# Rotary self-attention of a two-layer perceiver: units reordered by half of the tokens, output summed over heads in PSUM, scores on 64 keys instead of 128

## The chip, the cores and the metric

One core of a Trainium2 chip runs the whole program: TensorE (PE in the profile; its weight loads are PEld), VectorE (DVE), ScalarE (ACT), GpSimd (POOL) and SyncE (SP, which only issues DMAs here). The metric is the device time of one execution in microseconds, median of several runs.

## The reference, cut to what matters

The program is two layers, each of cross-attention, self-attention and a feed-forward net, on 16 batches of 64 tokens with 256 features. The change touches one block only, the self-attention of layer 1:

```python
N_HEADS, D_MODEL, D_HEAD = (16, 256, 128)
# x: (16, 64, 256), normalised; per head h:
q, k, v = xn @ W_Q[h] + b_Q[h], xn @ W_K[h] + b_K[h], xn @ W_V[h] + b_V[h]
q, k = apply_rope(q, cos, sin), apply_rope(k, cos, sin)
p = softmax(causal(q @ k.T / sqrt(128)))       # within one batch: 64 x 64
x += sum over h of (p @ v) @ W_O[h]  + b_O
```

## The kernel before

The 1024 tokens are 8 tiles of 128 rows; a tile holds two batches of 64. `self_attention_rotary` works in **units**: one head for one half of the tokens (`TH` = 4 tiles, 512 tokens), 32 units in all. Before, unit n is head n // 2 and half n % 2, so two units in a row share the weights of a head.

Every engine runs the same chain of steps 0 to 34 in a software pipeline (`unit_loop`; the order on each engine is written out by hand in its `step`). In step n there stand: the projections of unit n (Q and K with rotation, V), the scores and softmax of unit n - 1, the mix (probabilities times V) of unit n - 2, and the output projection of unit n - 3. Semaphores count finished steps; a wait blocks all that is behind it on its engine.

- PE, step n: `project_to` for Q (six f16 matmuls of 512 columns, since hi and lo parts of both operands are multiplied in three products), scores (f32, one per tile, over all 128 keys of the tile), `project_to` for K, transposes of the probabilities, output projection (12 matmuls), V (24 matmuls), mix.
- DVE: `rope` for Q, mask and row minimum of the scores, `rope` for K, addition of the output projection to `m.x`, reciprocal, `z_lo` (which signals `mix_kept`).
- ACT: in every second step `split_high` (L1694, f16 high part `w_hi` of the next head's weights), then the copy `probs_t` of the transposed probabilities, the four exponentials, the copy of V, `z_hi`.
- POOL: two additions of the rotation, the multiplication of the probabilities by the inverse sum, `split_low` (L1587, `w_lo`).
- SP: `load` fetches the raw weights of a head into one of two buffers `ra_raw` (384 KB), the biases of Q and K, and the bias of V (`ra_v_bias`). The three stand in one queue in this order, each behind its own wait: the raw weights wait for `split_low` two heads back (`w_split`), the Q/K bias for `rope` (`crossing`), the V bias for `z_lo` (`mix_kept`).

The mask is a 128 x 128 table; keys of the other batch of a tile have -1e30 in it. The output projection of each unit goes to its own PSUM group and DVE adds it to `m.x` in every step.

## Time and profile before

| | us |
|---|---|
| median of 3 runs | 900.21 |
| lowest, highest | 896.24, 904.9 |
| span of the profiled execution | 899.1 |
| PE, DVE busy in the span | 758.3, 644.4 |
| ACT, POOL busy in the span | 432.0, 404.5 |
| first weight split of the changed block starts | 597.8 |
| last addition of the block to `m.x` starts | 851.21 |

The profiled execution is one execution. Its own device time is not listed apart; its span, from the first to the last instruction, is 1.1 us under the median of the runs. The changed block takes 254 of the 899 us. Matmuls overlap in PE, so that PE's progress is read from the starts of its rows, not from their durations. In the timeline "x8" merges eight instructions; an f32 matmul appears as two.

### The profile page before, as it was taken

To read this page: it belongs to the slowest core of one execution; us is meant where nothing else is said; L and a number is where in the kernel's file an instruction comes from. 1 tells how busy PE (TensorE), PEld (TensorE's weight loads), DVE (VectorE), ACT (ScalarE), POOL (GpSimd) and SP (SyncE) were. 2 spreads that over 40 slices of the span, in tenths; PEclk is the share of its full clock that TensorE was granted. 3 is DMA by queue.
4 is the path that set the end of the run, shared out by engine and by line. 5 is a ranking of instruction groups with operands and counts; after the bars stand their busy time and mean duration, and the time that the engine had idled before them with its cause. 6 is when DMAs were issued, how large, how long until landed. Compare 5 with 4: busy or idle time off the path is not lost. (4 is left out here: it accounts for less than half of the span.)

```text
span 899.1 us, 17172 instructions
## 1 busy us (share of the span) xinstructions
PE 758.3 (84%) x5344; PEld 518.4 (58%) x5344; DVE 644.4 (72%) x1461; ACT 432.0 (48%) x1269; POOL 404.5 (45%) x318
## 2 busy tenths in 40 slices
PE   5997999677655579999998699868999999999776
PEld 4664666466422345444443467536788888888544
DVE  4356677656378865556556566658999999999767
ACT  2456655142244335454545656315555555555484
POOL 4301444326034227566566444439665656565210
PEclk9998999888868789999999899979999999999979
DMA  9352000000020011111100400001010101001101
GB/s 260 104 173 94 1 0 0 1 1 1 10 82 0 1 55 46 46 47 45 45 1 0 142 1 0 0 18 37 19 35 18 35 18 35 18 18 69 74 0 48
DMA packets 26638, 35.90 MB, mean 40 GB/s; under 512 B 10208, under 2 KB 17888, under 8 KB 25696
## 3 DMA queue, kind: packets, MB, share of 16 engines
q1 hardware_dynamic: 26592, 35.33, 12.6%
q8 instruction: 24, 0.39, 0.2%
q14 instruction: 22, 0.18, 0.1%
HBM read 34.27 MB, written 1.05 MB: 39 GB/s over the span
## 5 line engine op out<-in xcount | busy, mean ns | idle before, releaser
L1260 POOL TENSOR_TENSOR r_turned_lo<-r_turned_q,r_turned_hi 128x1024 f16<-128x1024 f32 x48 | 102.0, 2128 | 67.3 <-ACT r_turned_hi L1387 62.9
L1602 POOL TENSOR_TENSOR ra_direct<-ra_direct,ra_crossed 128x512 f32<-128x512 f32 x64 | 81.5, 1273 | 86.8 <-DVE ra_crossed L1746 86.8
L636 ACT ACTIVATE c_probs<-bank,c_neg_max 128x128 f32<-128x128 f32 x256 | 89.9, 377 | 60.1 <-DVE c_neg_max L688 60.0
L1746 DVE SCALAR_TENSOR_TENSOR ra_crossed<-bank,ra_bias,ra_sin 64x512 f32<-64x512 f32 x128 | 96.0, 750 | 1.9
L655 POOL TENSOR_TENSOR c_probs<-c_probs,c_inverse 128x512 f32<-128x512 f32 x64 | 65.3, 1039 | 70.9 <-DVE c_inverse L670 70.9
L1387 ACT ACTIVATE r_turned_hi<-r_turned_q 128x1024 f16<-128x1024 f32 x48 | 50.7, 1056 | 79.2 <-DVE r_turned_q L1434 79.1
L252 DVE TENSOR_TENSOR l_q_stack<-bank,l_q_stack 64x512 f16<-64x512 f32 (+1 forms) x64 | 44.1, 689 | 53.8 <-ACT l_q_stack L244 52.6
L601 PE MATMUL bank<-l_out_mat,c_ctx_t 128*128 128x256 f32 x256 | 61.8, 385 | 8.5 <-DVE c_ctx_t L699 8.5
L688 DVE TENSOR_REDUCE c_neg_max<-bank 128x4 f32<-128x512 f32 x64 | 41.4, 685 | 27.5 <-PE bank L65 27.5
L1705 ACT ACTIVATE ra_probs_t<-bank 128x512 f32<-128x512 f32 x32 | 19.1, 597 | 85.6 <-PE bank L1651 85.6
L601 PEld LDWEIGHTS bank<-l_out_mat,c_ctx_t 128*128 128x128 f32 x256 | 46.2, 190 | 18.4 <-issue 8.4
L636 ACT ACTIVATION_READ_ACCUMULATOR c_probs<-bank,c_neg_max 128x1 f32 x256 | 55.6, 217 | 0.0
L1710 ACT ACTIVATE ra_probs<-ra_masked,ra_neg_max 128x128 f32<-128x128 f32 x128 | 49.8, 390 | 11.7 <-DVE ra_neg_max L1765 11.3
L65 PE MATMUL bank<-xt_hi,ra_w_hi 128*128 128x512 f16 x128 | 49.3, 385 | 4.3 <-POOL ra_w_lo L1587 4.3
L1746 DVE SCALAR_TENSOR_TENSOR ra_direct<-bank,ra_bias,ra_cos 128x512 f32<-128x512 f32 x64 | 47.8, 746 | 6.7 <-PE bank L65 5.8
L680 DVE COPY c_probs_t<-bank 128x512 f32<-128x512 f32 x64 | 41.5, 685 | 14.7 <-PE bank L592 14.7
L65 PE MATMUL bank<-xt_lo,ra_w_hi 128*128 128x512 f16 x128 | 49.3, 385 | 0.0
L65 PE MATMUL bank<-xt_hi,ra_w_lo 128*128 128x512 f16 x128 | 49.2, 385 | 0.0
L244 ACT ACTIVATE l_q_stack<-bank 64x512 f16<-64x512 f32 (+1 forms) x64 | 37.6, 588 | 22.3 <-PE bank L65 16.8
L1332 PE MATMUL bank<-r_turned_hi,r_fold_hi 128*128 128x512 f16 x96 | 36.6, 382 | 11.2 <-POOL r_turned_lo L1260 11.1
L65 PE MATMUL bank<-kvt_hi,l_q_stack 128*128 (+1 forms) x256 | 35.1, 228 | 11.9 <-ACT c_probs L636 5.6
L100 POOL TENSOR_TENSOR all_rstd<-all_var,minus_half 128x4 f32<-128x4 f32 (+2 forms) x14 | 13.9, 993 | 69.1 <-DVE all_var L94 69.0
(239 smaller groups left out, 2233.7 us busy)
## 6 DMA issues: line engine op xcount, KB each, us to landing
ra_raw<-l_attn_w_dram SPq DMA_DIRECT2D x16, 384.0 KB, 3.0
wq<-l_wq_dram SPq DMA_DIRECT2D x16, 256.0 KB, 2.7
wo<-l_wo_dram SPq DMA_DIRECT2D x16, 256.0 KB, 3.3
wkcq<-l_wkcq_dram SPq DMA_DIRECT2D x16, 192.0 KB, 2.8
ra_wo<-l_attn_wo_dram SPq DMA_DIRECT2D x1, 2048.0 KB, 9.8
wqr<-l_wqr_dram SPq DMA_DIRECT2D x8, 192.0 KB, 3.5
x_res<-x_dram SPq DMA_DIRECT2D x2, 512.0 KB, 4.1
wkv<-l_wkv_dram SPq DMA_DIRECT2D x16, 64.0 KB, 3.0
```

What stands on the lines that cost most here:

```text
L65: mm = nc.tensor.matmul(out, lhs, rhs, start=(n == 0), stop=(n == last))
L252: nc.vector.tensor_tensor(m.q_stack[HD:P, at[0], at[1], :], src[e * HD:(e + 1) * HD], m.q_stack[0:HD, at[0], at[1], :], ALU.subtract).then ...
L601: mm = nc.tensor.matmul(out_bank, ctx_t[:, n, :, :].rearrange("p b s -> p (b s)"), m.out_mat[:, n, :], start=(n == 0), stop=(n == PAIRS - 1))
L636: e = nc.scalar.activation(probs[u][:, n, :], score_bank[q][:, n - q * HP, :], ACT.Exp, bias=neg_max[u][:, n:n + 1], accum_out=total[u][:, ...
L655: nc.gpsimd.tensor_tensor(out=probs[u][:, at, :], in0=probs[u][:, at, :], in1=inverse[u][:, at].unsqueeze(2).broadcast_to([P, HP, L]), op= ...
L680: nc.vector.tensor_copy(probs_t[u][:, at, :], turn_bank[q]).then_inc(turn_kept, 1)
L688: nc.vector.tensor_reduce(neg_max[u][:, at], score_bank[q], AX.X, ALU.max, negate=True).then_inc(maxed, 1)
L1260: nc.gpsimd.tensor_tensor(out=turned_lo[k % NCH][:], in0=turned_q[k % NCH][:], in1=turned_hi[k % NCH][:], op=ALU.subtract).then_inc(turned ...
L1387: nc.scalar.activation(turned_hi[k % NCH][:], turned_q[k % NCH][:], ACT.Copy).then_inc(turned_high, 1)
L1602: nc.gpsimd.tensor_tensor(out=direct[e][k][:], in0=direct[e][k][:], in1=crossed[k][:], op=ALU.add).then_inc(roped, 1)
L1710: ins = nc.scalar.activation(probs[1 - e][:, t, :], masked[1 - e][:, t, :], ACT.Exp, bias=neg_max[1 - e][:, t:t + 1], scale=-1.0, accum_ou ...
L1746: ins = nc.vector.scalar_tensor_tensor(dst[out_lo:out_lo + rows].rearrange("p t (b s) -> p (t b) s", b=2), src[lo:lo + rows], bias[v][lo:l ...
```

## The change

Units are ordered by halves: unit n is head n % 16 of half n // 16. So every unit needs the weights of another head, and each head's weights are loaded and split twice (32 loads of 384 KB, 32 splits on ACT and on POOL; there are now four buffers each for `w_hi` and `w_lo`, still two for `ra_raw`). The output projection of the 16 heads of a half is summed in two PSUM banks, and DVE adds them to `m.x` once for each half. Scores are computed for the 64 keys of the own batch only: eight f32 matmuls of 64 x 64 which put two tiles beside each other in the partitions of a PSUM bank; mask, exponentials and the multiplication by the inverse then run on 64 columns per tile. One transpose serves two tiles; the transposed blocks are copied into a `probs_t` whose other blocks were cleared once. Mask and minimum become two DVE instructions for all four tiles, with a wait between them. SP's loads are written out instead of looped.

```diff
-        w_hi = [sb(f"w_hi{v}", [P, 3, CC, P], F16) for v in range(2)]
-        w_lo = [sb(f"w_lo{v}", [P, 3, CC, P], F16) for v in range(2)]
+        w_hi = [sb(f"w_hi{f}", [P, 3, CC, P], F16) for f in range(4)]
+        w_lo = [sb(f"w_lo{f}", [P, 3, CC, P], F16) for f in range(4)]
...
-        masked = [sb(f"masked{f}", [P, TH, P]) for f in range(2)]
-        probs = [sb(f"probs{f}", [P, TH, P]) for f in range(2)]
-        probs_t = sb("probs_t", [P, TH, P])
+        masked = [sb(f"masked{f}", [P, TH, S]) for f in range(2)]
+        probs = [sb(f"probs{f}", [P, TH, S]) for f in range(2)]
+        probs_t = sb("probs_t", [P, TH, 2, S])
...
-        score_bank = g.bank[3][:].rearrange("p (t n) -> p t n", t=TH)
-        turn_bank = g.bank[4][:].rearrange("p (t n) -> p t n", t=TH)
+        score_bank = g.bank[3][:, 0:TH * S].rearrange("p (t n) -> p t n", t=TH)
+        turn_bank = g.bank[4][:, 0:TH * S]
...
+                step(n, n % 4, 0, 0)
+            with eng.Fori(1, H // 4) as i:
                 for f in range(4):
-                    step(4 * i + f, f, i)
+                    step(4 * i + f, f, i, 0)
+            for n in range(H, H + 4):
+                step(n, n % 4, n // 4, 1)
+            with eng.Fori(H // 4 + 1, UNITS // 4 - 1) as i:
+                for f in range(4):
+                    step(4 * i + f, f, i, 1)
...
+            def load(n, v, head):
                 w = 1 - v
-                if not isinstance(h, int) or h < H:
+                if not isinstance(n, int) or n < UNITS:
                     sp.wait_ge(loaded[v], 16)
-                    sp.wait_ge(w_split, h - 1)
-                    sp.dma_start(raw[v][:], a["l1_attn_w"][h]).then_inc(loaded[v], 16)
-                if not isinstance(h, int) or 3 <= h <= H:
+                    sp.wait_ge(w_split, n - 1)
+                    sp.dma_start(raw[v][:], a["l1_attn_w"][head(0)]).then_inc(loaded[v], 16)
+                if not isinstance(n, int) or 3 <= n <= UNITS:
                     sp.wait_ge(bias_loaded[w], 16)
-                    sp.wait_ge(crossing, 4 * (h - 2))
-                    sp.dma_start(bias[w][:], a["l1_attn_b"][h - 1]).then_inc(bias_loaded[w], 16)
-                if not isinstance(h, int) or h >= 4:
+                    sp.wait_ge(crossing, 2 * n - 4)
+                    sp.dma_start(bias[w][:], a["l1_attn_b"][head(1)]).then_inc(bias_loaded[w], 16)
+                if not isinstance(n, int) or n >= 4:
                     sp.wait_ge(v_bias_loaded[v], 16)
-                    sp.wait_ge(mix_kept, 2 * (h - 3))
-                    sp.dma_start(v_bias[v][:], a["l1_attn_bv"][h - 2]).then_inc(v_bias_loaded[v], 16)
-            for h in (2, 3):
-                load(h, h % 2)
-            with sp.Fori(2, H // 2) as i:
-                for v in range(2):
-                    load(2 * i + v, v)
-            for h in (H, H + 1):
-                load(h, h % 2)
+                    sp.wait_ge(mix_kept, n - 3)
+                    sp.dma_start(v_bias[v][:], a["l1_attn_bv"][head(2)]).then_inc(v_bias_loaded[v], 16)
+            for n in range(2, UNITS + 2):
+                load(n, n % 2, lambda behind: (n - behind) % H)
...
+            nc.gpsimd.memset(probs_t[:], 0.0).then_inc(cleared, 1)
+            def split_low(n, f):
+                pool.wait_ge(w_high, n + 1)
+                nc.gpsimd.tensor_tensor(out=w_lo[f][:], in0=raw[f % 2][:], in1=w_hi[f][:],
                                         op=ALU.subtract).then_inc(w_split, 1)
             split_low(0, 0)
+            split_low(1, 1)
...
-                following = next_head(n, f, i)
-                if following:
-                    split_low(*following[:2])
+                if not isinstance(n, int) or n + 2 < UNITS:
+                    split_low(n + 2, (f + 2) % 4)
...
+            def output(n, e, half):
+                pe.wait_ge(mix_kept, n - 2)
+                pe.wait_ge(wo_low, 1 if isinstance(n, int) and n < 4 else 4)
+                first, last = (isinstance(n, int) and (n - 3) % H == at for at in (0, H - 1))
+                if first:
+                    wait(pe, added, 2 * (n // H))
+                head = (n - 3) % H if isinstance(n, int) else n - 3 - half * H
+                for q in range(TP):
+                    for k in range(2):
+                        hi, lo = (z[1 - e][:, 2 * q + k, :] for z in (z_hi, z_lo))
+                        factors = split_factors(hi, lo, wo_hi[:, head, :], wo_lo[:, head, :])
+                        for j, (lhs, rhs) in enumerate(factors):
+                            mm = nc.tensor.matmul(out_bank[q][:, k, :], lhs, rhs,
+                                                  start=(first and k == 0 and j == 0),
+                                                  stop=(last and j == len(factors) - 1), skip_group_check=True)
+                mm.then_inc(summed, 1)
...
+                rows = slice(half * TH, (half + 1) * TH)
                 if project:
-                    if e == 0:
-                        pe.wait_ge(w_split, 2 * i + v + 1)
-                    project_to(n, v, rows, 0)
+                    pe.wait_ge(w_split, n + 1)
+                    project_to(n, f, rows, 0)
                 if score:
                     pe.wait_ge(roped, 2 * n)
-                    wait(pe, maxed, n - 1)
+                    wait(pe, limited, n - 1)
                     for t in range(TH):
-                        mm = nc.tensor.matmul(score_bank[:, t, :], direct[1 - e][0][:, t, :],
-                                              direct[1 - e][1][:, t, :], start=True, stop=True)
+                        for b in range(2):
+                            at, k = slice(b * S, (b + 1) * S), t % 2
+                            mm = nc.tensor.matmul(score_bank[k * HD:(k + 1) * HD, t - k + b, :], direct[1 - e][0][:, t, at],
+                                                  direct[1 - e][1][:, t, at], start=True, stop=True)
...
+                    for q in range(TP):
+                        mm = nc.tensor.transpose(turn_bank[:, q * P:(q + 1) * P],
+                                                 probs[e][:, 2 * q:2 * q + 2, :].rearrange("p t n -> p (t n)"),
+                                                 m.ident[:])
                     mm.then_inc(turned, 1)
                 if out:
-                    pe.wait_ge(mix_kept, n - 2)
-                    pe.wait_ge(wo_low, 1 if isinstance(n, int) and n < 4 else 4)
-                    head = out_head(n, f, i)
-                    for q in range(2):
-                        wait(pe, added, 2 * (n - 4) + q + 1)
-                        for t in range(2):
-                            mm = accumulate(nc, out_bank[q][:, t, :], split_factors(
-                                z_hi[1 - e][:, 2 * q + t, :], z_lo[1 - e][:, 2 * q + t, :],
-                                wo_hi[:, head, :], wo_lo[:, head, :]))
-                        mm.then_inc(out_done, 1)
+                    output(n, e, half)
...
+            def split_high(n, f, trips):
+                act.wait_ge(loaded[f % 2], 16 * trips)
+                wait(act, v_done, n - 3)
+                nc.scalar.activation(w_hi[f][:], raw[f % 2][:], ACT.Copy).then_inc(w_high, 1)
+            def step(n, f, i, half):
                 project, score, mix, out = stages(n)
                 e = f % 2
-                following = next_head(n, f, i)
-                if following:
-                    split_high(*following)
+                if not isinstance(n, int) or n + 2 < UNITS:
+                    split_high(n + 2, (f + 2) % 4, 2 * i + f // 2 + 2)
                 if mix:
                     act.wait_ge(turned, n - 1)
                     wait(act, mixed, n - 2)
-                    nc.scalar.activation(probs_t[:], turn_bank, ACT.Copy).then_inc(turn_kept, 1)
+                    for b in range(2):
+                        at = slice(b * HD, (b + 1) * HD)
+                        ins = nc.scalar.activation(probs_t[at, :, b, :], turn_bank[at].rearrange("p (a s) -> p a s", a=TH), ACT.Copy)
+                    ins.then_inc(turn_kept, 1)
...
+                    act.wait_ge(v_bias_loaded[e], 16 * (2 * i + f // 2))
+                    nc.scalar.activation(z_hi[e][:].rearrange("p t n -> p (t n)"), mix_bank,
+                                         ACT.Identity, bias=v_bias[e][:]).then_inc(z_high, 1)
...
+                    wait(dve, exped, n - 2)
+                    dve.wait_ge(tables, 64)
+                    dve.wait_ge(scored, n)
+                    nc.vector.scalar_tensor_tensor(masked[1 - e][:], score_bank, -SCALE,
+                                                   mask[:, 0:S].unsqueeze(1).broadcast_to([P, TH, S]),
+                                                   ALU.mult, ALU.add).then_inc(limited, 1)
+                    dve.wait_ge(limited, n)
+                    nc.vector.tensor_reduce(neg_max[1 - e][:], masked[1 - e][:], AX.X, ALU.min).then_inc(maxed, 1)
                 if project:
-                    rope(n, e, v, i, 1)
-                if out:
-                    u = 1 - e
-                    for q in range(2):
-                        dve.wait_ge(biased, 1)
-                        dve.wait_ge(out_done, 2 * (n - 3) + q + 1)
-                        at = slice(u * TH + 2 * q, u * TH + 2 * q + 2)
-                        wait(dve, added, 2 * (n - 4) + q + 1)
...
+                if isinstance(n, int) and n >= 3 and (n - 3) % H == H - 1:
+                    dve.wait_ge(biased, 1)
+                    dve.wait_ge(summed, n - 2)
+                    for q in range(TP):
+                        at = slice((n - 3) // H * TH + 2 * q, (n - 3) // H * TH + 2 * q + 2)
...
-    causal = np.where((block[:, None] == block[None, :]) & (row[None, :] <= row[:, None]),
-                      0.0, -1e30).astype(np.float32)
+    causal = np.where(row[None, :] <= (row % S)[:, None], 0.0, 1e30).astype(np.float32)
```

How the instructions stand now, at three places. The order prints the semaphores by the first of the names that share a register; the sentences say which they are here.

**SP, steady state.** Before, one pass for a head (buffer 0) in the loop. The wait `c0_out` is `w_split`, `c0_ln_turned` is `crossing`, `sa_exped0` is `mix_kept`:

```order
L1556 ISA [waits ra_loaded0]
L1557 ISA [waits c0_out]
L1557 DMA ra_raw<-l_attn_w_dram 128x768
L1560 ISA [waits ra_bias_loaded1]
L1561 ISA [waits c0_ln_turned]
L1561 DMA ra_bias<-l_attn_b_dram 128x2
L1564 ISA [waits ra_v_bias_loaded0]
L1565 ISA [waits sa_exped0]
L1565 DMA ra_v_bias<-l_attn_bv_dram 128x1
```

After, one unit; `sa_inverted0` is `mix_kept` now:

```order
L1562 DMA ra_raw<-l_attn_w_dram 128x768 [waits c0_out,ra_loaded1]
L1566 DMA ra_bias<-l_attn_b_dram 128x2 [waits c0_ln_turned,ra_bias_loaded0]
L1570 DMA ra_v_bias<-l_attn_bv_dram 128x1 [waits sa_inverted0,ra_v_bias_loaded1]
L1562 DMA ra_raw<-l_attn_w_dram 128x768 [waits c0_out,ra_loaded0]
L1566 DMA ra_bias<-l_attn_b_dram 128x2 [waits c0_ln_turned,ra_bias_loaded1]
L1570 DMA ra_v_bias<-l_attn_bv_dram 128x1 [waits sa_inverted0,ra_v_bias_loaded0]
```

The same three DMAs in the same order, but one group for each unit instead of one for two units; the raw weights of unit n + 1 stand behind the V bias whose wait is `mix_kept` of step n - 2, that is, the end of DVE's step n - 2.

**ACT, loop body.** Before, from `z_hi` of one step to V's copy of the next, and `z_hi` again, in a step without a split (`sa_maxed0` is `mixed`, `sa_scored0` is `turned`, `c0_ln_rstd` is `v_done`; `L51` and `REGISTER_ALU` rows only compute and test such counts):

```order
L1724 ACTIVATE ra_z_hi<-bank,ra_v_bias 128x512 [waits ra_v_bias_loaded1]
L1705 ACTIVATE ra_probs_t<-bank 128x512 [waits sa_maxed0,sa_scored0]
L1710 ACTIVATE ra_probs,ra_total<-ra_masked,ra_neg_max 128x128 [waits sa_scored0,sa_qk_done]
L1710 ACTIVATE ra_probs,ra_total<-ra_masked,ra_neg_max 128x128 x3
L1715 REGISTER_ALU
L1717 ACTIVATE ra_v<-bank 128x512 [waits sa_maxed0,c0_ln_rstd]
L51 REGISTER_ALU [waits sa_maxed0]
L1724 ACTIVATE ra_z_hi<-bank,ra_v_bias 128x512 [waits ra_v_bias_loaded1,sa_inverted1]
```

After, from `z_hi` to `z_hi` (`ra_loaded1` is the arrival of the raw weights, `sa_exped0` is `mixed` and `sa_scored1` is `turned` now):

```order
L1729 ACTIVATE ra_z_hi<-bank,ra_v_bias 128x512 [waits ra_v_bias_loaded0]
L1698 ACTIVATE ra_w_hi<-ra_raw 128x768 [waits c0_ln_rstd,ra_loaded1]
L1710 ACTIVATE ra_probs_t<-bank 64x4x64 [waits sa_exped0,sa_scored1]
L1710 ACTIVATE ra_probs_t<-bank 64x4x64
L1716 ACTIVATE ra_probs,ra_total<-ra_masked,ra_neg_max 128x64 [waits sa_scored1,sa_v_done]
L1716 ACTIVATE ra_probs,ra_total<-ra_masked,ra_neg_max 128x64 x3
L1721 REGISTER_ALU
L1723 ACTIVATE ra_v<-bank 128x512 [waits sa_exped0,c0_ln_rstd]
L1729 ACTIVATE ra_z_hi<-bank,ra_v_bias 128x512 [waits ra_v_bias_loaded1,sa_normed1,sa_exped0]
```

`ra_w_hi<-ra_raw` now opens every step, ahead of the two `probs_t` copies and the exponentials. In step n it is the split for unit n + 2.

**PE, scores and transposes in the loop.** Before:

```order
L65 MATMUL bank<-xt_hi,ra_w_lo 128x512
L1642 MATMUL bank<-ra_direct 128x128 [waits sa_qk_done,c0_ln_hi]
L1642 MATMUL bank<-ra_direct 128x128 x3
L65 MATMUL bank<-xt_hi,ra_w_hi 128x512 [waits c0_ln_turned]
...
L1651 MATMUL bank<-ident_sb,ra_probs 128x128 [waits sa_scored1,sa_v_kept]
L1651 MATMUL bank<-ident_sb,ra_probs 128x128 x3
```

After:

```order
L65 MATMUL bank<-xt_hi,ra_w_lo 128x512
L1656 MATMUL bank<-ra_direct 64x64 [waits sa_qk_done,c0_ln_hi]
L1656 MATMUL bank<-ra_direct 64x64 x7
L65 MATMUL bank<-xt_hi,ra_w_hi 128x512 [waits c0_ln_turned]
...
L1665 MATMUL bank<-ident_sb,ra_probs 128x128 [waits sa_maxed0,sa_scored0]
L1665 MATMUL bank<-ident_sb,ra_probs 128x128
```

Eight 64x64 score matmuls stand where four 128x128 stood, and two transposes where four stood; the projections around them are as before.

## Rows read from the trace of the kernel before

**Rows 1.** Windows of the whole core: busy us of each engine, then PEclk, DMA share and GB/s.

```profile
400.00:440.00 40.00, 37.48 (x191) 18.11 (x190) 24.53 (x44) 19.48 (x32) 24.03 (x12) 1.00 0.17 51
640.00:820.00 180.00, 180.00 (x1633) 144.92 (x1631) 176.84 (x433) 93.52 (x276) 104.81 (x84) 1.00 0.09 24
```

**Rows 2.** Timeline of PE, one step: start us, us, what.

```profile
705.30 1.05 PE L1642 MATMUL bank<-ra_direct 128*128 128x128 f32 x8
706.19 0.38 PE L65 MATMUL bank<-xt_hi,ra_w_hi 128*128 128x512 f16 x1
...
707.49 0.60 PE L1651 MATMUL bank<-ident_sb,ra_probs 128*128 128x128 f32 x4
707.92 0.27 PE L65 MATMUL bank<-ra_wo_hi,ra_z_hi 128*128 x1
...
712.81 1.05 PE L1642 MATMUL bank<-ra_direct 128*128 128x128 f32 x8
```

**Rows 3.** Timeline of DVE in the same step.

```profile
705.06 0.75 DVE L1788 SCALAR_TENSOR_TENSOR ra_z_lo<-bank,ra_v_bias,ra_z_hi 128x512 f16<-128x512 f32 x1
...
708.03 0.29 DVE L1765 CUSTOM_DVE_ANT_0 ra_masked<-bank,ra_mask 128x128 f32<-128x128 f32 x1
...
708.88 0.08 DVE L1765 DVE_READ_ACCUMULATOR2_ANT ra_neg_max<- 128x1 f32 x1
...
711.19 1.29 DVE L1779 TENSOR_TENSOR x_res<-x_res,bank 128x512 f32<-128x512 f32 x2
```

**Rows 4.** Timeline of ACT in the same stretch.

```profile
704.34 0.69 ACT L1724 ACTIVATE ra_z_hi<-bank,ra_v_bias 128x512 f16<-128x512 f32 x1 [0.49 <-PE bank L1677]
704.93 0.83 ACT L1694 ACTIVATE ra_w_hi<-ra_raw 128x768 f16<-128x768 f32 x1
...
709.00 0.40 ACT L1710 ACTIVATE ra_probs<-ra_masked,ra_neg_max 128x128 f32<-128x128 f32 x1 [0.28 <-DVE ra_neg_max L1765]
...
709.40 0.39 ACT L1710 ACTIVATE ra_probs<-ra_masked,ra_neg_max 128x128 f32<-128x128 f32 x1
...
711.86 0.69 ACT L1724 ACTIVATE ra_z_hi<-bank,ra_v_bias 128x512 f16<-128x512 f32 x1 [0.49 <-PE bank L1677]
...
719.96 0.83 ACT L1694 ACTIVATE ra_w_hi<-ra_raw 128x768 f16<-128x768 f32 x1
```

**Rows 5.** Timeline of SP's queue: DMA issues, in two stretches.

```profile
700.63 0.33 SPq L1557 DMA_DIRECT2D ra_raw<-l_attn_w_dram  x1
...
705.98 0.33 SPq L1565 DMA_DIRECT2D ra_v_bias<-l_attn_bv_dram  x1
...
825.98 0.33 SPq L1565 DMA_DIRECT2D ra_v_bias<-l_attn_bv_dram  x1
826.35 0.42 SPq L1575 DMA_DIRECT2D gf_raw<-l_gate_dram  x1
```

**Rows 6.** The tile `ra_raw`, last line of its view.

```profile
DMA to landing us min/median/max: 2.8/3.0/4.9
```

**Rows 7.** ACT's groups by shape: busy us, mean ns of one.

```profile
L1717 ACT ACTIVATE ra_v<-bank 128x512 f32<-128x512 f32 x32 | 19.1, 597 | 11.5 <-PE bank L65 8.8
...
L1729 ACT ACTIVATE ra_wo_hi<-ra_wo 128x1024 f16<-128x1024 f32 x4 | 4.2, 1049 | 0.0
```

**Rows 8.** POOL's split of the weights, groups by shape.

```profile
L1587 POOL TENSOR_TENSOR ra_w_lo<-ra_raw,ra_w_hi 128x768 f16<-128x768 f32 x16 | 26.3, 1644 | 5.7 <-ACT ra_w_hi L1694 5.7
```

**Rows 9.** Timeline of PE, projection of the rotary layer: matmuls in column and row tiles.

```profile
402.47 1.90 PE L1297 MATMUL bank<-wkr,wqr 64*128 64x64 f32 x16
404.30 0.39 PE L1332 MATMUL bank<-r_turned_hi,r_fold_hi 128*128 128x512 f16 x1
...
406.69 0.38 PE L65 MATMUL bank<-xt_hi,r_big_lo 128*128 128x512 f16 x1
407.00 0.65 PE L1304 MATMUL bank<-wo,wkv 128*64 128x256 f32 x4
407.58 0.39 PE L1332 MATMUL bank<-r_turned_hi,r_fold_hi 128*128 128x512 f16 x1
```

More of the change, by code:

```diff
@@ L1574, in _ @@
             for k, name in enumerate(("l1_gate", "l1_up", "l1_down")):
                 sp.dma_start(m.gf_raw[:, k, :], a[name]).then_inc(g.gf_loaded, 16)
-        def next_head(n, f, i):
-            if f % 2 or (isinstance(n, int) and n // 2 + 1 >= H):
-                return None
-            return (2 * i + 1, 1, i + 1) if f == 0 else (2 * i + 2, 0, i + 2)
         @block.gpsimd
         def _(pool):
-            def split_low(h, v):
-                pool.wait_ge(w_high, h + 1)
-                nc.gpsimd.tensor_tensor(out=w_lo[v][:], in0=raw[v][:], in1=w_hi[v][:],
+            nc.gpsimd.memset(probs_t[:], 0.0).then_inc(cleared, 1)
@@ L1620, in _, with project_to @@
         def _(pe):
-            def project_to(n, v, rows, k):
+            def project_to(n, f, rows, k):
                 wait(pe, crossing, 2 * n + k - 1)
@@ L1668, in step @@
                         for c in range(CC):
-                            xs = [x[:, c, e * TH + t, :] for x in (m.xt_hi, m.xt_lo)]
-                            factors += split_factors(*xs, w_hi[v][:, 2, c, :], w_lo[v][:, 2, c, :])
+                            xs = [x[:, c, half * TH + t, :] for x in (m.xt_hi, m.xt_lo)]
+                            factors += split_factors(*xs, w_hi[f][:, 2, c, :], w_lo[f][:, 2, c, :])
                         mm = accumulate(nc, v_bank[:, t, :], factors)
@@ L1690, in _, with step @@
         def _(act):
-            def split_high(h, v, trips):
-                act.wait_ge(loaded[v], 16 * trips)
-                wait(act, v_done, 2 * (h - 1))
-                nc.scalar.activation(w_hi[v][:], raw[v][:], ACT.Copy).then_inc(w_high, 1)
-            def step(n, f, i):
+            act.wait_ge(cleared, 1)
+            def split_high(n, f, trips):
+                act.wait_ge(loaded[f % 2], 16 * trips)
+                wait(act, v_done, n - 3)
+                nc.scalar.activation(w_hi[f][:], raw[f % 2][:], ACT.Copy).then_inc(w_high, 1)
+            def step(n, f, i, half):
                 project, score, mix, out = stages(n)
                 e = f % 2
-                following = next_head(n, f, i)
-                if following:
-                    split_high(*following)
+                if not isinstance(n, int) or n + 2 < UNITS:
+                    split_high(n + 2, (f + 2) % 4, 2 * i + f // 2 + 2)
                 if mix:
@@ L1731, in _ @@
             split_high(0, 0, 1)
+            split_high(1, 1, 1)
             unit_loop(act, step)
```

68 lines of the change are left out of this document (23 added, 45 removed).

## The prediction

> **What bounds the kernel now.** I read first the windows of the changed block. In its steady part PE is shown busy for 180.00 of 180 us, DVE for 176.84, ACT for 93.52 and POOL for 104.81, with the granted clock at 1.00, the 2.4 GHz level [rows 1]. So either PE or DVE sets the pace. The timeline of PE decides. Its starts follow each other without a gap: scores at 705.30, K projection at 706.19, transposes at 707.49, output projection at 707.92, and the scores of the next step at 712.81 [rows 2]. A step takes 7.51 us and PE is full. DVE has 3 us of slack in 24 steps [rows 1], under 2%: it is a second bound just behind. ACT is idle half the time. SP's queue is never late. A V bias goes out 0.17 us after `z_lo` (705.06 + 0.75 = 705.81 [rows 3], issue at 705.98 [rows 5]). The raw weights issued at 700.63 [rows 5] land about 3.0 us later [rows 6], at 703.6; the two buffers alternate, the split at 704.93 is that of the other one, and these weights serve the split at 719.96 [rows 4], 16 us later. In the code the arrival is needed three steps on.
>
> **What the change takes off.** DVE loses the two additions to `m.x`, 1.29 us as shown [rows 3], in 30 of 32 steps. Its mask part takes 0.85 us now (708.03 to 708.88 [rows 3]) and becomes one instruction of 256 columns and one reduction of as many. For each I take 0.4 to 0.5 us, between half and all of a 512-column instruction at 0.75; with the wait in between 0.9, so this is even. DVE falls to about 6.3 us per step. That alone gives nothing, since PE is full. PE loses two of four transposes: 707.92 - 707.49 = 0.43 [rows 2], so 0.22 us. ACT's exponentials have 64 columns fewer each. From 512 to 1024 columns an ACT instruction grows from 597 to 1049 ns [rows 7], 0.88 ns per column, so each is 0.06 shorter and the four go from 1.56 (4 x the 0.40 from 709.00 to 709.40, less the rounding [rows 4]) to 1.33 us. POOL pays 1.64 us [rows 8] once a step where it paid once in two, +0.8 less what half a multiplication saves, on 104.81 / 24 = 4.4 us per step [rows 1]: at most 5.2, hidden.
>
> **Scores on PE.** Before, 706.19 - 705.30 = 0.89 us [rows 2]. After, eight f32 matmuls of 64 x 64 in column tiles, 16 instructions. The trace has no such row, so I bound it. Low: if both column halves run together and nothing else costs, half of 0.89, 0.45 us. High: the nearest burst, 16 f32 instructions of 64 columns with tile shapes changing, takes 404.30 - 402.47 = 1.83 [rows 9] with 0.09 ahead of it: 1.92 us. The gap ahead is seen at the column-tiled pair too: the last 512-column matmul starts at 406.69 and would release the array at 406.91 (0.216 each, 1.30 for six [rows 2]), but the tiled one starts at 407.00. Inside that pair the four instructions of 256 columns take 0.58 to the next matmul where eight instructions of 128 columns, as many columns in all, take 0.89 [rows 2, 9], so column tiles do overlap. In the changed code four instructions in a row go to one column tile before the other gets its four, so there is little to overlap. I take 1.5 us, nearest to the burst less its four inner shape changes. PE's step is then 7.51 - 0.22 + 0.61 = 7.90 us (6.85 to 8.32 with the bounds).
>
> The Trainium skill, TensorEngine Tiling (Array Packing), section Key Properties, says that tiles execute independently, and that changing the tiling mode drains TensorE. The rows agree with both: the overlapped pair, and some 0.09 us at the entry. Its section Theoretical Speedup gives up to 2x for a dimension of 64; by that the scores would be at the low bound, which leaves the sum below as it is and feeds a rival.
>
> **The transfer that is moved.** This is the term that counts. SP's queue keeps its order, raw weights, Q/K bias, V bias, but now goes through it once per step. The raw weights of unit n + 1 stand behind the V bias that waits for `mix_kept` >= n - 3, which `z_lo` of step n - 2 signals. They are wanted by `split_high` at the top of ACT's step n - 1. Before there were three steps for it; now there is none. ACT waits there in order, and behind that wait are queued the two `probs_t` copies (PE's mix waits for them), the exponentials (DVE's reciprocal, then POOL), V's copy, and `z_hi`, for which DVE's `z_lo` waits, which releases the next transfer. The loop closes on itself, and its length is a step. From the end of `z_lo`:
>
> - V bias out after 0.17 [rows 3, 5], raw weights issued 0.37 behind it (825.98 to 826.35, the same two-in-a-row [rows 5]): 0.54
> - landing 3.0, bounds 2.8 and 4.9 [rows 6]
> - ACT takes up the semaphore and a register test: 0.10, between the 0.04 from DVE's last mask row (708.88 + 0.08) to the exponential at 709.00 [rows 3, 4] and the 0.17 above
> - `w_hi`: 0.83, of which 0.10 overlaps with the next, as 704.34 + 0.69 and 704.93 show [rows 4]: 0.75
> - two copies of 256 columns for one of 512: 0.597 - 0.22 = 0.37 each, 0.27 to 0.30 with the overlap: 0.60 for both (up to 1.2 if half a height costs all)
> - exponentials 1.33 and the last sum: 1.38
> - V's copy 0.60 - 0.10 [rows 7]: 0.50
> - `z_hi` 0.69 and hand-over [rows 4]: 0.72
> - `z_lo` 0.75 [rows 3]
>
> Sum 0.54 + 3.0 + 0.10 + 0.75 + 0.60 + 1.38 + 0.50 + 0.72 + 0.75 = **8.34 us** against 7.51. PE's 7.90 lies under it with 0.44 to spare and DVE's 6.3 with 2. The mix isn't late in it: `probs_t` is there 5.0 us after `z_lo`, 1.0 us of mix ends at 6.2, and `z_hi` comes at 6.9.
>
> The loop holds from the raw weights of unit 5 to those of unit 31: 27 steps. 27 x 0.83 = +22.4 us. The start adds the clearing of `probs_t` ahead of the first split and a second 1.64 us split on POOL [rows 8] ahead of its first rotation, partly behind PE: +1.0, bounds 0 and 2. At the end one step without a transfer, lighter for DVE: -0.3. The next block's weights, issued at 826.35 now [rows 5], go out at `z_lo` of step 31; three steps and the next norm still lie behind that, so nothing; if that cover were gone it would be the 3 us of a landing. Sum +23 us. The profiled span of 899.1 becomes 922; it stood 1.1 under the median, so **923 us**.
>
> Bounds: with landing 2.8 and no cost of the register test 8.0 us, +14; with a landing of 3.3 beside the V bias, copies at 0.9 and exponentials at 1.5, 9.1 us, +43. One landing of 4.9 costs 2 us once.
>
> **The rivals.**
> - *The weights are there in time and PE bounds.* For it: SP's wait could be over sooner than I think if ACT has slack after all. Against it: the row order and the 3.0 of [rows 6]. Then the step is 7.6 (scores at 1.2): 32 x 0.09 + 1 = +4, 904 us.
> - *Faster: column tiles overlap fully.* Scores at 0.45 make PE's step 6.85, DVE's 6.3 follows, and 30 x 0.66 = 20 us go, less 1 at the start: 881 us. It decides only where the loop above is shorter than 7.51, that is with a landing under 3.0 - 0.83 = 2.2 us. The shortest of the trace is 2.8. Somewhat over that, 7.2 us a step, gives 891.
> - *Scores dearer than the burst.* Eight first instructions, each unhidden, make PE's step 8.6: 32 x 1.09 + 1 = +36, 936 us.
> - *PE waits so much that its clock falls.* In the stretch at 400 PE was shown busy 37.48 of 40 us, with waits, at a granted clock of 1.00 [rows 1]; here it idles 0.44 of 8.34 by my sum. At the 1.2 GHz level PE's step would near 15 us; not likely, and far outside.
>
> **How the numbers follow.** The self-closing loop 0.72 (910 to 942), dearer scores 0.08 (930 to 950), PE alone 0.11 (902 to 914), faster 0.06, clock 0.03. No change that a measurement of this kernel can tell is within 1%, 9 us: 891 to 909. Slower by over 1%: 0.72 + 0.08 + 0.03 and a small part of the third, less the low tail of the first: 0.82. Same 0.12, faster 0.06. The range takes the first case and the middle of the third: 905 to 941.
>
> **What would show it.** In the profile after: the starts of `w_hi` are 8.3 us apart, each idle for about 3.6 us before it with DMA or SP as releaser; `ra_raw` is issued about 0.5 us after every `z_lo`; DVE shows about 6.3 busy per step and waits before `z_lo` for ACT; PE shows a gap before the mix. Wrong would be: `w_hi` starting right behind `z_hi`, PE without gaps, or scores that take over 2 us from their first row to the next projection.

## The result and the profile after

The changed kernel takes **932.1 us** (929.6 to 935.6, 4 runs) against 900.7 (896.2 to 904.9, 4 runs) for the kernel before on the same chip: ratio 1.034, 95% interval 1.030 to 1.038. That is slower, as forecast, and inside the predicted range: +31 us where the working had +23. Runs over 1.5% above the fastest of their kernel are left out of all ratios; they are three of the 49 of the kernel before in the experiments below (910 to 911 us) and two of the ten of the narrow scores alone (1857 and 4014 us).

The windows over the steady part of the block, to be held against [rows 1], show no engine full any more: PE is busy 178.82 of 210 us, and DVE fell from 98% to 70%.

```profile
640.00:850.00 210.00, 178.82 (x1785) 131.17 (x1781) 147.68 (x243) 98.44 (x312) 114.18 (x97) 0.99 0.17 46
```

The totals of the waits in the same stretch (engine, line, releaser: us in all, times, longest) name one wait on a transfer and, behind it, waits of PE and DVE on ACT, the engine that waited for it. POOL's wait on DVE costs nothing, since nobody waits for POOL here:

```profile
ACT ra_w_hi L1698 <- DMA ra_raw<-l_attn_w_dram: 109.9, 24, 5.5
POOL ra_direct L1599 <- DVE ra_crossed L1752: 86.3, 48, 2.7
...
DVE ra_inverse L1785 <- ACT ra_probs L1716: 34.0, 23, 2.4
PE bank L1684 <- ACT ra_probs_t L1710: 31.2, 23, 2.3
DVE ra_z_lo L1789 <- ACT ra_z_hi L1729: 25.8, 25, 1.3
```

ACT's timeline of one step, answering to [rows 4], has the whole chain; "idle before" stands in brackets:

```profile
722.52 0.84 ACT L1698 ACTIVATE ra_w_hi<-ra_raw 128x768 f16<-128x768 f32 x1 [4.41 <-DMA ra_raw<-l_attn_w_dram]
...
731.16 0.84 ACT L1698 ACTIVATE ra_w_hi<-ra_raw 128x768 f16<-128x768 f32 x1 [4.49 <-DMA ra_raw<-l_attn_w_dram]
731.91 0.75 ACT L1710 ACTIVATE ra_probs_t<-bank 64x256 f32<-64x256 f32 x2
732.69 0.35 ACT L1716 ACTIVATE ra_probs<-ra_masked,ra_neg_max 128x64 f32<-128x64 f32 x1
...
734.15 0.60 ACT L1723 ACTIVATE ra_v<-bank 128x512 f32<-128x512 f32 x1
734.64 0.68 ACT L1729 ACTIVATE ra_z_hi<-bank,ra_v_bias 128x512 f16<-128x512 f32 x1
```

SP's queue in the same step (compare [rows 5]): the V bias, and the raw weights 0.42 us behind it.

```profile
727.53 0.33 SPq L1570 DMA_DIRECT2D ra_v_bias<-l_attn_bv_dram  x1
727.95 0.38 SPq L1562 DMA_DIRECT2D ra_raw<-l_attn_w_dram  x1
...
736.18 0.33 SPq L1570 DMA_DIRECT2D ra_v_bias<-l_attn_bv_dram  x1
```

DVE's timeline closes the loop: `z_lo` ends at 726.71 + 0.75 = 727.46, the V bias is issued at 727.53; the next `z_lo` begins at 735.36.

```profile
726.71 0.75 DVE L1789 SCALAR_TENSOR_TENSOR ra_z_lo<-bank,ra_v_bias,ra_z_hi 128x512 f16<-128x512 f32 x1 [1.02 <-ACT ra_z_hi L1729]
...
735.36 0.75 DVE L1789 SCALAR_TENSOR_TENSOR ra_z_lo<-bank,ra_v_bias,ra_z_hi 128x512 f16<-128x512 f32 x1 [1.02 <-ACT ra_z_hi L1729]
```

PE's timeline: a gap of 1.18 us before the mix, for which the two copies of `ra_probs_t` come late, and the scores, which are over 0.67 us after they start.

```profile
722.67 0.22 PE L65 MATMUL bank<-ra_w_hi,xt_lo 128*128 128x128 f16 x1
724.07 1.16 PE L1684 MATMUL bank<-ra_probs_t,ra_v 128*128 128x128 f32 x8 [1.18 <-ACT ra_probs_t L1710]
...
726.14 0.38 PE L65 MATMUL bank<-xt_hi,ra_w_lo 128*128 128x512 f16 x1
726.45 0.73 PE L1656 MATMUL bank<-ra_direct 128*64 128x64 f32 x16
727.12 0.39 PE L65 MATMUL bank<-xt_hi,ra_w_hi 128*128 128x512 f16 x1
```

**Where the time lies.** The first rotation of a step on DVE (the row `ra_direct` behind each `z_lo`) marks the steps. From the first to the last of the 32 marks the kernel before takes 230.0 us (603.3 to 833.3, median step 7.51), the changed one 261.5 (604.0 to 865.5, median 8.65). That is +31.5; ahead of the first mark +0.6, behind the last -1.5: +30.6 in all, as the spans have it (929.7 against 899.1). Below, "step" is the median distance of these marks and "block" the first to the last.

### The profile page after: what moved, and what is told of

It is laid out like the page before. It is cut to its first block and busy times, and to the rows that moved or that the text cites. A ratio compares the mean times of both kernels' runs of the same rounds, so it can differ in the third digit from the quotient of the medians.

```text
span 929.7 us, 17201 instructions
## 1 busy us (share of the span) xinstructions
PE 753.1 (81%) x5533; PEld 499.9 (54%) x5536; DVE 603.4 (65%) x1209; ACT 439.3 (47%) x1317; POOL 416.7 (45%) x335
## 5 line engine op out<-in xcount | busy, mean ns | idle before, releaser
L1698 ACT ACTIVATE ra_w_hi<-ra_raw 128x768 f16<-128x768 f32 x32 | 26.8, 842 | 128.7 <-DMA ra_raw<-l_attn_w_dram 127.1
L1684 PE MATMUL bank<-ra_probs_t,ra_v 128*128 128x128 f32 x256 | 37.6, 291 | 32.5 <-ACT ra_probs_t L1710 32.3
L1583 POOL TENSOR_TENSOR ra_w_lo<-ra_raw,ra_w_hi 128x768 f16<-128x768 f32 x32 | 52.5, 1643 | 1.0 <-ACT ra_w_hi L1698 1.0
L1684 PEld LDWEIGHTS bank<-ra_probs_t,ra_v 128*128 128x128 f32 x256 | 31.8, 196 | 36.9 <-ACT ra_probs_t L1710 36.8
L1789 DVE SCALAR_TENSOR_TENSOR ra_z_lo<-bank,ra_v_bias,ra_z_hi 128x512 f16<-128x512 f32 x32 | 24.0, 751 | 34.2 <-ACT ra_z_hi L1729 34.2
```

Of the source, the lines that this page charges most:

```text
L1583: nc.gpsimd.tensor_tensor(out=w_lo[f][:], in0=raw[f % 2][:], in1=w_hi[f][:], op=ALU.subtract).then_inc(w_split, 1)
L1684: mm = nc.tensor.matmul(mix_bank[:, t * P:(t + 1) * P], v_sb[(f + 2) % 4][:, t, :], probs_t[:, t, :, :].rearrange("p b s -> p (b s)"), sta ...
```

## The experiments

Each is timed beside runs of the kernel before on its own chip. Their medians over all runs are 901.4 us for the first four experiments, 902.3 for the next four and 899.0 for the last.

**The transfer put ahead of the wait.** The changed kernel, but SP issues the next raw weights before it waits for the V bias's buffer.

```diff
-                    sp.dma_start(raw[v][:], a["l1_attn_w"][head(0)]).then_inc(loaded[v], 16)
...
+                if n + 1 < UNITS:
+                    load_raw(n + 1)
                 if not isinstance(n, int) or n >= 4:
                     sp.wait_ge(v_bias_loaded[v], 16)
                     sp.wait_ge(mix_kept, n - 3)
```

> The changed kernel with one thing moved: in SP's queue the raw weights of unit n + 1 go out ahead of the V bias that waits for z_lo of step n - 2, behind their own wait (the split of unit n - 1 on POOL, a step earlier). Theory A, the loop z_lo - V bias - raw weights - split - exponentials - z_hi - z_lo sets the step: the idle time of ACT before w_hi goes, and the step falls from 8.65 us to what PE needs, 7.51 - 0.22 (two transposes) - 0.13 (scores, by the trace after) = 7.16 us, or a little over: 27 x 1.5 = 40 us less than the changed kernel, some 890 us, about 1% under the kernel before. Theory B, PE or ACT has too much work a step after the change (column tiles, twice the splits): the step stays at 8.65 and the time at 932.

Measured: 892.5 us, ratio 0.989 (0.982 to 0.995). Step 7.17, block 222.7. PE is full again, DVE is not:

```profile
640.00:820.00 180.00, 180.00 (x1863) 135.25 (x1861) 152.57 (x251) 104.31 (x320) 117.90 (x100) 1.00 0.20 54
```

On ACT the split now follows `z_hi` at once, with no bracket behind it:

```profile
707.23 0.69 ACT L1733 ACTIVATE ra_z_hi<-bank,ra_v_bias 128x512 f16<-128x512 f32 x1 [0.35 <-PE bank L1688]
707.82 0.83 ACT L1702 ACTIVATE ra_w_hi<-ra_raw 128x768 f16<-128x768 f32 x1
```

So the place of one transfer behind that wait costs 39 us of block (261.5 - 222.7), and all the rest of the change together gains 7 (230.0 - 222.7). PE's step is the old one less what the rows say: 7.51 - 0.22 (transposes) - 0.13 (scores, 0.76 from the end of Q's projection for 0.89) = 7.16.

**A dose in the loop.** The changed kernel with two more DMAs of 0.5 KB, of which nothing is read, issued between V bias and raw weights.

```diff
                     sp.wait_ge(w_split, n - 1)
+                    if n >= 5:
+                        for _ in range(2):
+                            sp.dma_start(spare[:, 2 * n + _:2 * n + _ + 1], a["l1_attn_bv"][head(0)]).then_inc(spared, 16)
                     sp.dma_start(raw[v][:], a["l1_attn_w"][head(0)]).then_inc(loaded[v], 16)
```

> The changed kernel with two more DMAs of 0.5 KB (to a spare tile that nobody reads) issued just ahead of the raw weights of each unit from 5 on. Theory A: each delays the raw weights by one issue, 0.38 to 0.42 us, so the loop grows by 0.8 us in 27 steps: +21 to +23 us on the changed kernel, some 954 us. Theory B: the queue is not on the path, nothing changes, 932 us. The computation is the same.

Measured: 959.2 us, ratio 1.064 (1.056 to 1.071), where some 954 were expected; step 9.76, block 290.9, 29.4 more than the changed kernel's. Whatever is put between `z_lo` and the raw weights' arrival comes back once a step, which a bound elsewhere would have absorbed. In the step shown, the weights go out 1.33 us behind the V bias, 0.91 more than above, and ACT takes them up 3.32 after the issue:

```profile
726.30 0.33 SPq L1574 DMA_DIRECT2D ra_v_bias<-l_attn_bv_dram  x1
726.72 0.86 SPq L1565 DMA_DIRECT2D ra_spare<-l_attn_bv_dram  x2
727.63 0.43 SPq L1566 DMA_DIRECT2D ra_raw<-l_attn_w_dram  x1
```

```profile
730.95 0.84 ACT L1702 ACTIVATE ra_w_hi<-ra_raw 128x768 f16<-128x768 f32 x1 [5.51 <-DMA ra_raw<-l_attn_w_dram]
```

The 27 passes from `z_lo` to `z_lo` take 9.81 us on the mean against 8.74 in the changed kernel, 1.07 more: 0.91 for the two issues, 0.14 for landing and take-up (3.44 for 3.29), 0.02 for a `z_hi` that comes late. These are 28.9 of the 29.4 us. The expectation had only the issues, at 0.8.

PE's clock (the figure ahead of the DMA share) is no longer at the 2.4 GHz level throughout. The mix takes 1.4 to 2.1 us for the usual 1.16 in 6 of the 27 passes; only in three of them does `z_hi` wait for it, by 0.2 to 0.3 us. So the clock adds 0.7 us to the loop in all.

```profile
640.00:880.00 240.00, 190.81 (x1810) 137.63 (x1807) 151.70 (x248) 100.12 (x315) 116.08 (x98) 0.95 0.17 42
```

**The order by halves alone.** The order and queue of the first experiment, with the scores, mask, transposes and copies of the kernel before (128 keys).

```diff
-                        for b in range(2):
-                            at, k = slice(b * S, (b + 1) * S), t % 2
-                            mm = nc.tensor.matmul(score_bank[k * HD:(k + 1) * HD, t - k + b, :], direct[1 - e][0][:, t, at],
-                                                  direct[1 - e][1][:, t, at], start=True, stop=True)
+                        mm = nc.tensor.matmul(score_bank[:, t, :], direct[1 - e][0][:, t, :],
+                                              direct[1 - e][1][:, t, :], start=True, stop=True)
...
-                    for q in range(TP):
-                        mm = nc.tensor.transpose(turn_bank[:, q * P:(q + 1) * P],
...
+                    for t in range(TH):
+                        mm = nc.tensor.transpose(turn_bank[:, t, :], probs[e][:, t, :], m.ident[:])
...
+                    nc.scalar.activation(probs_t[:], turn_bank, ACT.Copy).then_inc(turn_kept, 1)
```

> Halves of the tokens, output summed over heads in PSUM and raw weights ahead of the V bias as in the run before, but scores, mask, transposes and probabilities over 128 keys as in the kernel before. PE's work per step is that of the kernel before, 7.51 us; DVE's is 1.2 us less. Theory A with PE as the bound of the kernel before: the step stays 7.5 us, 899 to 903 us. If DVE had been the bound before and PE only looked full: the step falls towards 7 us, 885 us.

Measured: 903.5 us, ratio 1.000 (0.996 to 1.005). Step 7.52, block 233.1 where the kernel before has 230.0; 2.9 of the 3.1 us lie in the first five steps. DVE is busy for 149.7 of 180 us instead of 176.8, and that buys nothing while PE is full:

```profile
640.00:820.00 180.00, 180.00 (x1631) 145.07 (x1630) 149.74 (x387) 101.95 (x289) 123.16 (x96) 1.00 0.19 52
```

**The narrow scores alone.** The kernel before in its own order, with scores on 64 keys, two transposes and two copies (the lines of the last diff, the other way round).

> The kernel before with the narrow scores alone: 64 keys, one transpose for two tiles, mask and minimum in two DVE instructions; heads in the old order, additions to x every step, old loads. PE needs 7.16 us a step, DVE 2 x 2.27 + 0.8 + 1.2 + 0.18 + 0.66 = 7.4 us. If DVE is a second bound just behind PE: step 7.4 to 7.5, 897 to 900 us, hardly a gain. If PE alone was the bound: step 7.2, 890 us. If the column tiles themselves cost time on PE: 905 us or more.

Measured: 895.5 us (8 runs), ratio 0.994 (0.990 to 0.997). Step 7.33, block 224.9.

```profile
640.00:820.00 180.00, 178.15 (x1816) 132.00 (x1816) 175.74 (x295) 93.40 (x303) 97.92 (x87) 1.00 0.09 25
```

The expectation was a step of 7.4 to 7.5 and 897 to 900 us, so both came out a little lower. PE alone would do 7.17; here DVE, which keeps the additions to `m.x`, is at 98% and sets 7.33. Its only wait over these 180 us is one of 0.5 us; in the first experiment it waited 23.6 us for `z_hi`. The narrow scores are worth 0.18 us a step by themselves, the sum in PSUM nothing by itself, and the two together 0.34.

**The order of the column tiles.** The first experiment's kernel, in which two matmuls (four instructions) go to one column tile, then two to the other, rewritten in two ways: the tile changes from matmul to matmul (first piece of the diff), or all of one tile comes before the other (second).

```diff
-                    for t in range(TH):
-                        for b in range(2):
-                            at, k = slice(b * S, (b + 1) * S), t % 2
+                    for q in range(TP):
+                        for b, k in ((0, 0), (0, 1), (1, 0), (1, 1)):
+                            at, t = slice(b * S, (b + 1) * S), 2 * q + k
...
-                    for t in range(TH):
+                    for t in (0, 2, 1, 3):
```

> The kernel with the raw weights ahead, and the eight score matmuls in another order: the column tile changes after each matmul instead of after every second. PE is full there (step 7.17 us), so the scores' time shows in the step. They take 0.77 us from the end of the Q projection to the start of the K projection, 0.09 of it at the entry. If what is left is overlap that the order limits: 0.65 to 0.7 us, step 7.05 to 7.1, some 3 us less. If both column tiles already keep each other busy as well as they can: no change, 892 us.

> The same kernel with the score matmuls grouped: all four of the lower column tile, then all four of the upper. If the cheapness of the scores (0.77 us where the forecast had 1.5) comes from the two column tiles running at once: hardly any overlap is left, 16 x 0.058 or more, 0.95 to 1.9 us in all, and the step grows to 7.35 or more, +6 us at the least. If column tiles have nothing to do with it: no change, step 7.17.

Measured: alternating 888.7 us, ratio 0.984 (0.980 to 0.988); grouped 900.8, ratio 0.998 (0.995 to 1.002). Steps 7.13 and 7.41, against 7.17. PE's timeline of the first experiment's kernel, then of alternating, then of grouped:

```profile
722.46 0.38 PE L65 MATMUL bank<-xt_hi,ra_w_lo 128*128 128x512 f16 x1
722.76 0.73 PE L1660 MATMUL bank<-ra_direct 128*64 128x64 f32 x16
723.43 0.39 PE L65 MATMUL bank<-xt_hi,ra_w_hi 128*128 128x512 f16 x1
```

```profile
721.70 0.69 PE L1660 MATMUL bank<-ra_direct 128*64 128x64 f32 x16
722.32 0.39 PE L65 MATMUL bank<-xt_hi,ra_w_hi 128*128 128x512 f16 x1
```

```profile
720.92 0.97 PE L1660 MATMUL bank<-ra_direct 128*64 128x64 f32 x16
721.82 0.39 PE L65 MATMUL bank<-xt_hi,ra_w_hi 128*128 128x512 f16 x1
```

First score to next projection: 0.67, 0.62 and 0.90 us. The step follows, -0.04 and +0.24, which says once more that PE sets it here. Alternating was expected at 7.05 to 7.1 us a step, so it gained a little less than that; grouped came as expected. The two times of alternating and of the first experiment can't be told apart (0.984, 0.980 to 0.988, and 0.989, 0.982 to 0.995): the gain is read from step and block (220.9 for 222.7).

Grouped, the burst costs as much as eight instructions of 128 columns did (0.89 [rows 2]), and the 0.09 us at the entry, which those did not have, come on top: the first score starts 0.09 after the last 512-column matmul would release the array (726.14 + 0.22 = 726.36 to 726.45 in the changed kernel). So the grouped order has no gain from column tiles. Whether that is because nothing overlaps, or because some overlap is eaten by a cost of each instruction, these runs do not separate. The Trainium skill, TensorEngine Tiling (Array Packing), section Theoretical Speedup, gives up to 2x for a dimension of 64. Here it is 0.89 / 0.62 = 1.44 at best, 0.89 / 0.71 = 1.25 with the entry, and the order of the instructions decides how much of it is had.

**The wait taken away by buffers.** The changed kernel with its queue order, but four V-bias buffers for two, so that SP waits for `mix_kept` two steps further back.

```diff
-                    sp.wait_ge(v_bias_loaded[v], 16)
-                    sp.wait_ge(mix_kept, n - 3)
-                    sp.dma_start(v_bias[v][:], a["l1_attn_bv"][head(2)]).then_inc(v_bias_loaded[v], 16)
+                    w = (n - 2) % 4
+                    if n >= 6:
+                        sp.wait_ge(v_bias_loaded[w], 16)
+                        sp.wait_ge(mix_kept, n - 5)
+                    sp.dma_start(v_bias[w][:], a["l1_attn_bv"][head(2)]).then_inc(v_bias_loaded[w], 16)
```

> The changed kernel with SP's order of DMAs as it is, but four buffers for the V bias instead of two, so that its load waits for z_lo two steps earlier. Theory A says that it is the wait ahead of the raw weights, not their place in the queue, that costs: step 7.2 us, 892 us, as with the raw weights moved ahead. If the place itself or the traffic of small DMAs ahead of the weights mattered: the step stays over 7.5 us.

Measured: 891.0 us, ratio 0.988 (0.984 to 0.992), step 7.17, block 222.8: the first experiment's within a tenth of a microsecond. It was neither the order in the queue nor the load itself, but the wait standing ahead of it. SP issues the weights when POOL's split has freed their buffer (700.46 + 1.64 = 702.10 on POOL's timeline), and they are read by the second `w_hi` from there:

```profile
702.18 0.33 SPq L1564 DMA_DIRECT2D ra_raw<-l_attn_w_dram  x1
```

```profile
706.76 0.83 ACT L1702 ACTIVATE ra_w_hi<-ra_raw 128x768 f16<-128x768 f32 x1
...
713.86 0.83 ACT L1702 ACTIVATE ra_w_hi<-ra_raw 128x768 f16<-128x768 f32 x1
```

That is 11.7 us between issue and use, for 3.0 of landing.

**The loop with the old scores.** The changed kernel's queue order and two buffers, with the 128-key scores of the third experiment.

> Halves of the tokens with SP's queue as in the changed kernel (raw weights behind the V bias), but scores over 128 keys as before. Theory A: the loop is 0.07 + 0.42 + 3.21 + 0.75 (split) + 0.50 (one copy of 512) + 1.7 (exponentials of 128) + 0.49 + 0.72 + 0.75 = 8.6 us, so the step is 8.6 to 8.7 and the time 930 to 935, although none of the narrow scores is in it. If the narrow scores or the column tiles had part in the loss: the step falls to 7.5 to 8.

Measured: 926.9 us (2 runs), ratio 1.027 (1.022 to 1.032); step 8.41, block 258.6. That is under the expected 8.6 to 8.7 and 930 to 935. The slowdown needs no narrow scores; they add 0.24 us to the median step, more than I had put down for them. ACT's timeline shows where:

```profile
726.78 0.84 ACT L1690 ACTIVATE ra_w_hi<-ra_raw 128x768 f16<-128x768 f32 x1 [4.51 <-DMA ra_raw<-l_attn_w_dram]
727.53 0.58 ACT L1700 ACTIVATE ra_probs_t<-bank 128x512 f32<-128x512 f32 x1
728.01 0.39 ACT L1705 ACTIVATE ra_probs<-ra_masked,ra_neg_max 128x128 f32<-128x128 f32 x1
```

One copy of full height takes 728.01 - 727.53 = 0.48 of the loop, the two of half height 732.69 - 731.91 = 0.78; the four exponentials give back 1.54 - 1.46 = 0.08. The blocks differ by 2.9 us only: in this trace four landings took 3.8 to 4.3 us (one in the changed kernel's), and the steps outside the loop are 1.6 us longer.

**Buffers and alternating tiles together.** The four V-bias buffers and the alternating tiles in one kernel; its diff is the two above.

> The changed kernel with its queue order, four V-bias buffers, and scores in which the column tile alternates from matmul to matmul: the two edits that gave most, together. Theory: the buffers take the wait out of the transfer loop, after which PE sets the step, and the alternation shortens PE's burst by 0.04 us of 7.17 as it did with the other order, 32 times 1.3 us in all; so a step of 7.13 and 888 to 890 us. Rival: with the transfers out of the way the difference between the two orders of SP's queue is in the start of the program alone, and the time falls anywhere between 886 and 892 with no gain from the alternation that its interval can tell.

Measured: 890.8 us (12 runs), ratio 0.991 (0.988 to 0.994), step 7.13 as expected, block 220.9; the time is just above the expected 888 to 890. In the trace the gain of 2 us in the block is there; in the time it can't be told from the four buffers alone. What the programs do ahead of the block is the same code in all of them, yet the block's first weight split starts at 593.1 to 602.5 us in the nine traces; a difference under 5 us is read from the block, not from the time. The version to keep is this one or the first experiment's with alternating tiles, 0.9% and 1.6% faster than the kernel before and about 4% to 5% faster than the change as made.

## Why the prediction was right, and where its sizes were off

**The mechanism was right.** The raw weights behind the V bias's wait, the loop from `z_lo` through SP, the landing and ACT's chain back to `z_lo`, and PE and DVE below it: the trace shows each link, moving the transfer or adding buffers removes the whole loss, and a dose put into it comes back in full. As forecast, `w_hi` waits for the DMA in every step of the loop, and the mix is not late in it (it starts at 732.72, and `z_hi` at 734.64 follows V's copy without a gap). DVE is busy 6.15 us a step (147.68 over 24 steps of 8.74) and POOL 4.75 (at most 5.2 forecast). The 6.3 forecast for DVE was not what its own rows gave: 176.84 / 24 - 1.29 + 0.05 = 6.13. Nor does the sign of being right, 3.6 us of idle time before `w_hi`, follow from the sum, which gives 0.03 + 0.75 + 0.54 + 3.10 = 4.4 from the end of `z_hi`; 4.49 was measured.

**The loop is 8.65 us, not 8.34.** Term by term, from the rows above, forecast first:

- out of `z_lo` to the issue of the weights: 0.54, measured 0.07 + 0.42 = 0.49
- landing and take-up: 3.10, measured 731.16 - 727.95 = 3.21
- `w_hi`: 0.75, measured 0.75
- two copies: 0.60, measured 0.78
- exponentials: 1.38, measured 734.15 - 732.69 = 1.46
- V's copy 0.50, `z_hi` 0.72, `z_lo` 0.75: measured 0.49, 0.72, 0.75

The copies are the largest miss, and the step that failed there is the overlap, not the duration. A copy of 64 partitions and 256 columns was costed at 0.37 us, and the 48 of them in the steady part measure 369 ns. But 0.07 to 0.10 was taken off each for the overlap with the next instruction, and two advance the queue by 0.78: they have none. The trace of the kernel before shows the same in another block: two copies of half height take their full 1.19 and the next starts behind them, while a copy of full height and 256 columns lets the next start 0.28 after its own start.

```profile
390.94 1.19 ACT L244 ACTIVATE l_q_stack<-bank 64x512 f32 x2
392.16 0.38 ACT L1382 ACTIVATE l_out_mat<-bank 128x256 f32 x1
392.44 1.05 ACT L1387 ACTIVATE r_turned_hi<-r_turned_q 128x1024 f16<-128x1024 f32 x1
```

Why half height loses the overlap was not tried. The upper bound of 1.2 for both copies was too high. The exponentials shrank by 0.02 each, not by 0.06. The landing is 0.11 longer with a small load just ahead; the view of the tile, against [rows 6], has

```profile
DMA to landing us min/median/max: 3.0/3.2/4.8
```

The median is 3.1 and 3.0 in the first experiment and with four buffers, where nothing goes out within 1 us ahead of the weights, and 3.4 with the dose.

**The mean is above the step shown.** Over the 27 steps of the loop the changed kernel takes 236.1 us, 8.74 each, the kernel before 203.5, 7.54 each: +32.6, where the working had 27 x 0.83 = 22.4. Of the 10.2 missing, 0.31 x 27 = 8.4 are the terms above, 2.5 the distance of 8.74 from 8.65, less 0.7 since the old step was 7.54 too. The 2.5 come almost all from the landing: from issue to `w_hi` the 27 passes take 3.05 to 4.21 us, 3.29 on the mean, for the 3.21 of the pass above. The longest of them gives 1.0. SP issued its weights at 788.88 and ACT took them at 793.09:

```profile
793.09 0.84 ACT L1698 ACTIVATE ra_w_hi<-ra_raw 128x768 f16<-128x768 f32 x1 [5.49 <-DMA ra_raw<-l_attn_w_dram]
```

PE was then idle for 2.26 us before the mix, and its clock fell to 0.50, the 1.2 GHz level, until about 798; the mix took 796.47 - 794.64 = 1.83 us for the usual 1.0. Little of that comes into the loop: `z_hi` starts 0.72 after V's copy instead of 0.49, and the pass from `z_lo` to `z_lo` takes 9.88 us, 1.0 for the landing and 0.23 for the mix above 8.65. The slow projection behind it holds up DVE's rotation by 0.62, so the marks show a step of 10.58 there and one of 7.87 after it. The timeline and the windows of that place:

```profile
794.64 2.04 PE L1684 MATMUL bank<-ra_probs_t,ra_v 128*128 128x128 f32 x8 [2.26 <-ACT ra_probs_t L1710]
796.47 0.63 PE L65 MATMUL bank<-xt_hi,ra_w_hi 128*128 128x512 f16 x1
```

```profile
792.00:794.00 2.00, 0.38 (x7) 0.20 (x4) 1.64 (x3) 0.91 (x2) 0.26 (x1) 1.00 0.02 6
794.00:796.00 2.00, 1.36 (x6) 1.36 (x7) 0.00 (x0) 1.96 (x10) 1.00 (x1) 0.68 0.00 0
796.00:798.00 2.00, 2.00 (x8) 1.01 (x7) 0.67 (x2) 1.33 (x3) 1.67 (x2) 0.50 0.01 4
```

So the rival of the falling clock was real, at one step in 27, and cost some 0.2 us. "One landing of 4.9 costs 2 us once" was right in kind: one of 4.2 cost 1.0.

**PE's scores were mis-sized, without harm to the number.** 1.5 us were taken, 0.76 came. The step that failed is the choice of the nearest row: the burst in [rows 9] also changes its row tiles, and its 1.83 us, less four shape changes, were taken over for instructions that share all 128 rows; the overlap of the pair beside it, which the prediction saw, was given up for the order. PE's step is 7.17, not 7.90. It lies under the loop either way, so the forecast does not show it, but the rival built on it was wrong in sign: with the weights in time the kernel does not go to 904 us, it goes to 891 to 893. The fast rival's low bound of 0.45 was not reached either, by alternating tiles with 0.62. That "faster" needs a landing under 2.2 us holds for the change as written; the prediction did not ask what moving the wait would give.

**Start and end.** +1.0 was taken for the start: it was +0.6 ahead of the first mark, within the spread of some 9 us there, and -0.2 over the first three steps. -0.3 was taken for the end: it was -1.0 in the last step and -1.5 behind the last mark. So the loop's 10.2 us too little is offset by 2.7 too little gain at the two ends, which is luck. What either end is due to was not tried.

**DVE.** The mask's two instructions were forecast even at 0.9 and take 0.80 (729.68 to the rotation at 730.48). Taking the additions off DVE gives nothing alone, as said, but it is needed for the narrow scores to pay in full: 7.33 us without it, 7.17 with it.

## What to carry to other kernels

A load queued behind a wait inherits that wait: follow what releases it, and if the load's user stands upstream of the releaser, the loop of latency and engine work is a step of its own, to be summed like any engine's. Such a loop leaves every engine partly idle, and two more buffers for the small tile (or one issue moved up) turned +3.4% into -1.2% (-1.1%). When a new layout splits one instruction into two of half the height, take from a row of that height what two in a row cost, the overlap too.

## What the chip showed that was not expected

- Height buys nothing on ACT, and half height loses the overlap: a copy of 64 x 256 lasts 369 ns and one of 128 x 256 383, but the first advances the queue by 0.39 us and the second by 0.28. One of 128 x 512 advances it by 0.48, two of 64 x 256 by 0.78. The exponential of 64 columns advances it by 0.365 with its accumulator read, that of 128 by 0.385.
- Sixteen f32 instructions of 64 x 64 score tiles take 0.62, 0.67 or 0.90 us by the order of the column tiles alone.
- The median landing of 384 KB is 3.0 to 3.1 us with nothing within 1 us ahead of it, 3.2 with one 0.5 KB load 0.42 us ahead, 3.4 with three.
- Idle gaps of 1.1 to 1.6 us before each mix leave PE's clock at 0.99 over 210 us; after one gap of 2.26 us it fell to the 1.2 GHz level for some 3 us. With the dose the gaps are 0.6 to 2.8 us and the mean clock is 0.95 over 240 us. The length of the gap alone does not decide: the mix was slow behind six gaps of 2.27 to 2.50 us, and at full speed behind one of 2.78.
